# ScalarE makes the masked scores of the attention two groups ahead, half before the factors and half behind them

## The reference, cut to what matters

```python
xs = (x @ W_src).reshape(N, HEADS, HID)
xd = (x @ W_dst).reshape(N, HEADS, HID)
a_src = jnp.einsum('nhc,hc->nh', xs, att_src)
a_dst = jnp.einsum('nhc,hc->nh', xd, att_dst)
e = jax.nn.leaky_relu(a_src[src] + a_dst[dst], NEG_SLOPE)
m = jax.ops.segment_max(e, dst, num_segments=N)
ee = jnp.exp(e - m[dst])
denom = jax.ops.segment_sum(ee, dst, num_segments=N)
alpha = ee / (denom[dst] + 1e-16)
msg = xs[src] * alpha[:, :, None]
out = jax.ops.segment_sum(msg, dst, num_segments=N)
```

## Time and profile before

| | us |
|---|---|
| median of 3 runs | 8418.5 (8417.85 to 8419.08) |
| the profiled execution: its own time | 8423.03 |
| its span, first to last instruction | 8421.2 |
| the attention in it | 7169 to about 8340 |

### The profile page before, as it was taken

How to read it: one execution, slowest core, us unless ns; L and a number is a source line. 1 busy time by engine, 2 the same in 40 slices (tenths; PEclk the granted TensorE clock), 3 DMA queues, 4 the chain that set the end, 5 groups by cost and what they waited for, 6 DMA issues and landing times. The chain is left out here.

```text
span 8421.2 us, 105716 instructions
## 1 busy us (share of the span) xinstructions
PE 5596.3 (66%) x23206; PEld 3877.0 (46%) x23206; DVE 5678.2 (67%) x15211; ACT 3349.2 (40%) x10636; POOL 6042.4 (72%) x6427
## 2 busy tenths in 40 slices
PE   5777746666666666776667775666655555788885
PEld 3444423333444444444444443444444444667664
DVE  8959138888666666666666665555544444888887
ACT  2333347777455552333333332000001111666665
POOL 2777767777677777777777777777777776766664
PEclk6555558888788888999899998888765666777877
DMA  2111144444222224444444445444433322211111
GB/s 75 59 57 59 59 117 119 119 119 120 74 63 63 63 61 143 119 119 118 125 132 119 119 119 130 124 116 116 116 84 62 62 61 56 53 48 49 49 48 38
DMA packets 632208, 749.11 MB, mean 89 GB/s; under 512 B 257044, under 2 KB 490152, under 8 KB 631448
## 3 DMA queue, kind: packets, MB, share of 16 engines
q0 software_dynamic: 239808, 572.66, 23.8%
q1 hardware_dynamic: 391496, 169.55, 8.0%
q10 hardware_dynamic: 272, 0.14, 0.0%
HBM read 617.05 MB, written 124.77 MB: 88 GB/s over the span
## 5 line engine op out<-in xcount | busy, mean ns | idle before, releaser
L824 DVE TENSOR_TENSOR acc<-acc,ps 128x256 f32 (+3 forms) x4704 | 1761.3, 374 | 1550.9 <-PE ps L1862 1254.2
L1145 POOL DMA_INDIRECT rows<-table_gcn,index_dst x1984 | 1889.1, 952 | 671.7 <-issue 570.9
L1862 PE MATMUL ps<-rows,hot 128*128 128x256 f32 (+2 forms) x5536 | 1506.2, 408 | 1254.3 <-DMA rows<-table_gcn,index_dst 467.6
L1862 PEld LDWEIGHTS ps<-rows,hot 128*128 128x128 f32 x5536 | 1097.3, 244 | 1652.6 <-issue 719.7
L1756 ACT ACTIVATE ut<-u,fld 128x128 f16<-128x128 f16 x1568 | 541.9, 392 | 1532.9 <-DVE u L1804 1531.8
L1145 POOL DMA_INDIRECT rows<-table_gat,index_dst x832 | 784.9, 943 | 379.6 <-issue 239.3
L1145 POOL DMA_INDIRECT rows<-table_mean,index_src x784 | 741.3, 946 | 249.2 <-issue 234.4
L1145 POOL DMA_INDIRECT rows<-table_lin,index_dst x784 | 739.9, 944 | 247.5 <-issue 234.7
L1114 PE MATMUL ps<-prod,hot 128*128 128x257 f32 x1568 | 592.1, 494 | 365.6 <-DVE acc L824 197.2
L1847 PE MATMUL ps<-prod,ut 128*128 128x392 f16 x3136 | 741.2, 365 | 0.0
L1145 POOL DMA_INDIRECT hot_v<-table_gcn,index_dst x576 | 548.3, 952 | 175.5 <-issue 163.6
(11 more groups left out here) (428 smaller groups left out, 11017.7 us busy)
## 6 DMA issues: line engine op xcount, KB each, us to landing
fld<-dst_rows SPq DMA_DIRECT2D x98, 544.0 KB
rows<-table_gcn,index_dst POOLq DMA_INDIRECT x1984
table_gcn<-acc SPq DMA_DIRECT2D x147, 128.0 KB
fld<-left_rows SPq DMA_DIRECT2D x147, 128.0 KB
pay<-dst_rows SPq DMA_DIRECT2D x832, 1.0 KB
rows<-table_gat,index_dst POOLq DMA_INDIRECT x832
rows<-table_lin,index_dst POOLq DMA_INDIRECT x784
rows<-table_mean,index_src POOLq DMA_INDIRECT x784
```

Source lines behind the costliest of these rows:

```text
L824: c.nc.vector.tensor_tensor(to, to, product, ALU.add).then_inc(c.added.sem, 1)
L1145: pool.indirect_dma_start(to(q, j), None, table, bass.IndirectOffsetOnAxis(ap=c.idx[k][:, t:t + 1], axis=0)).then_inc(c.gathered[q % per]. ...
L1862: pe.matmul(c.ps[:, bank(q, j), 0:used], c.hot[:, r % 2, j, :], row_of(c, s, r, j, used), start=True, stop=True).then_inc(c.mm.sem, 1)
```

## The change

ACT's body begins with the two exponentials of group q. Then stand `turned` of q+1, `mask8` and quarters 0 and 1 of group q+2, the factor of q+1, and quarters 2 and 3 of group q+2. Before the loop it makes all four quarters of group 1. Since `mask8` can now be written sooner after its last reader, it waits for that reader (`scaled` of the group before). No instruction's shape or number changes, and the other engines keep their order.

```diff
@@ masked @@
                 if b == 0:
                     act.wait_ge(c.hot_ready.sem, q + (c.hot_ready.n + 1))
+                    if not first(q):
+                        act.wait_ge(m.scaled.sem, q * 4 + m.scaled.n)
                     nc.scalar.activation(s.mask8[:, :, :], hot_of(r), ACT.Copy, scale=-1.0,
@@ body of ScalarE @@
                 q = RING * i + r
-                if nxt(i, r):
-                    for b in range(3):
-                        masked(*nxt(i, r), b)
                 act.wait_ge(m.scored.sem, q + (m.scored.n + 1))
                 nc.scalar.activation(weight8, s.z[:, :, :], ACT.Exp).then_inc(m.powered.sem, 1)
                 nc.scalar.activation(heads(s.wt)[:, :, :, CH], s.z[:, :, :], ACT.Exp).then_inc(m.kept.sem, 1)
                 if nxt(i, r):
-                    masked(*nxt(i, r), 3)
-
                     turned(*nxt(i, r))
+                for b in range(2):
+                    if nxt(i, r, 2):
+                        masked(*nxt(i, r, 2), b)
+                if nxt(i, r):
                     factor(*nxt(i, r))
+                for b in range(2, 4):
+                    if nxt(i, r, 2):
+                        masked(*nxt(i, r, 2), b)
@@ before the loop @@
             turned(0, 0)
             factor(0, 0)
+            for b in range(4):
+                masked(0, 1, b)
             written_out(AG, body, RING)
```

## The result

| | before | after |
|---|---|---|
| median of 4 runs | 8418.17 us (8416.84 to 8419.08) | 8345.67 us (8341.48 to 8350.73) |
| ratio, 95% interval | | 0.9911 [0.9900, 0.9923] |
| the profiled execution: time, span | 8423.03, 8421.2 | 8345.77, 8344.0 |

The kernel is 72.5 us faster, or 0.9%. The forecast was 8379.6, with a range from 8350 to 8398. The direction was right and the size was not: the gain is nearly twice the 38.9 us of the sum, and the time lies 4 us beyond the range. A repeat of the changed kernel on another chip gave 8342.63, so this is no accident of one run.

What follows compares the result with a forecast made beforehand. The prediction took a ring through DVE and ACT, with twelve blocks before the exponential, to set the attention's pace. Terms -47.7 + 0.5 + 0.3 + 8 = -38.9 us gave 8384.1, or 8379.6 us as a median; range 8350 to 8398.

Steps and rivals of the forecast that it cites:

- the ring: Attention's pace: product on DVE, maxima, `drop`, factor, mask, twelve blocks, exponential, product; mean step 11.22 us.
- The wait for the exponentials, -47.7 us: DVE's product: its 47.9 us of waits for ACT's exponentials go, all but the last group's 0.2 us.
- PE comes next: Quarter 0 of PE's transposes: at low clock some 0.25 us late for DVE's maximum, in up to 65 groups; plus 8 us.
- The start, +0.3 us: Start of the attention: first exponentials stand behind four more ACT blocks, so the first product comes 0.3 us later.
- the fetches, +0.5: POOL's queue: rows are needed one group earlier; 0 to 3 us allowed in the first dozen groups, 0.5 taken.
- ACT free in time, by 1.2 us: ACT's queue: blocks done by T + 8.5, next scores ready at T + 9.7 (T: product's start), leaving 1.2 us.
- The loss as half of the throttled time: PE's clock: the skill's rule would give 234 us lost; the prediction read 34 us from DVE's waits instead.
- the clock stays up: Rival: PE's idle spells behind ACT's blocks go and its clock never falls; -81 us, 8337; chance 0.15.
- The rival of the slower look-up: PE's look-up at low clock takes 1.6 us more, DVE waits 1.5; up to 8468; chances 0.14 part, 0.04 slower.

Runs made afterwards that it cites:

- e3: Changed kernel with all four quarters of ACT's blocks put behind the factor, none in front: 8547.00 us.
- e11: The changed kernel run once more, on the same chip as e9: 8342.63 us.
- e10: e4 with DVE's maximum of quarter 1 moved in front of its product: 8385.85 us against e4's 8446.27.
- e4: Changed kernel in which DVE makes four eighths of each one-hot matrix twice, about 0.7 us more DVE work a group: 8446.27 us.
- e2: Changed kernel with all four quarters of ACT's blocks for the group after next in front of the factor: 8344.02 us.
- e5: Changed kernel with three unread transposes added on PE between quarters 2 and 3 in each group: 8343.50 us.
- e9: Changed kernel with DVE's maximum of quarter 1 moved in front of its product, behind that of quarter 0: 8325.18 us.
- e6: Kernel before with three unread transposes added on PE between quarters 2 and 3 in each group: 8418.52 us.
- e8: Changed kernel in which DVE makes one eighth of each one-hot matrix twice, about 0.3 us more a group: 8392.47 us.
- e7: e4 with three unread transposes added on PE between quarters 2 and 3 in each group: 8437.05 us.
- e1: Kernel before, still one group ahead, with two quarters of ACT's blocks before the exponentials and two behind, not three and one: 8408.67 us.

## Why the prediction was right or wrong

- **The bound and the ring: right.** e3 lengthened the ring and the step grew as worked out; the changed kernel's timeline has the new order of events at the times laid out.
- **The wait for the exponentials, -47.7 us: right in kind, too small.** It went completely, but a full-clock group lost 0.64 us (10.83 to 10.19) and its recorded wait was 0.53. The record of the maximum before the product runs 0.08 us past the point at which the next instruction can start. The sum counted idle time from the end of that record. About 100 times 0.08 us is 8 us, and DVE's busy time in the attention, in which overlapping records count once, fell by 1034.61 - 1025.45 = 9.2 us, of which the shorter product (1212 in place of 1223 ns, 104 times) is 1.1. The Trainium skill, "Perfetto Trace Analysis", section "Summary: the profiler window per engine type", says that a record of VectorE runs until the write is acknowledged; the trace agrees, in that the next instruction starts 0.08 us before the record's end.
- **"PE comes next", +8 us: wrong, and this is the step that failed.** It said that falls of the clock stay as frequent at the same place, and that some of their cost is newly paid at quarter 0. Measured instead: behind the first groups no maximum but the fourth waits at all, so nothing is paid at quarter 0; and the fourth waits in 22 groups in place of 65. The maxima's waits fell by 23.5 us (41.6 to 18.1), and the look-up's waits rose by 0.9 (5.5 to 6.4). The term should have been about -23. Together with the 8 us above it makes up the difference: -47.7 - 8 - 23.5 + 0.9 = -78.3, against the 78.0 measured between the first and the last product. (That the two agree to 0.3 us is partly luck: idle spells too short to be printed grew by about 3 us before the maxima, and smaller changes make up for it.) The price at quarter 0 was misread as well. The prediction lets its transposes begin where the look-up's record ends, at 7832.24; in the trace of before they begin at 7832.09:

```profile
7832.09 0.63 PE L2432 MATMUL ps<-ident,hot_v 128*128 128x128 f32 x4
```

With 1.08 us at low clock they end at 7833.17, 0.07 us behind the start of the maximum and not 0.25.
- **The start, +0.3 us, and the fetches, +0.5:** the start was right: from ACT's first block to the first product it is 15.33 us in place of 15.11, 0.2 more. The fetches cost nothing: ACT's blocks waited 1.4 us for one, as before, at the first group only. That the first product came 0.8 us later (7185.3 in place of 7184.5), as much as both terms together, is luck: the other 0.6 us is a later start of the whole attention, which moves by microseconds from one execution to the next (in e11, the same kernel, the first product comes at 7182.3).
- **ACT free in time, by 1.2 us:** it waits 1.25 us in the group shown. Right.
- **The loss as half of the throttled time:** this rule of the Trainium skill, from "TensorE: Matmul & The Clock Gate", section "HAM oscillation — how this bites in real kernels", stood in the prediction against 34 us of waits. In this kernel the low clock has a price only where PE is waited for: e10 at 0.84 pays nearly nothing at the maxima, and e4 at 0.79 pays 44 us. The measurement stands against the rule here too.
- **The rival "the clock stays up"** (chance 0.15, 8337) is nearest to what happened: a gain beyond 52 us, though the clock did not stay up. It gave the removed spells behind ACT as the cause. e4 rules that out: the spells stay away and the waits come back. What the waits follow is the length of a group. As DVE's work grows from 0 to 0.3 to 0.7 us more, the waits grow from 18 to 35 to 52 us. Over all kernels, the groups of 102 in which quarter 3 takes over 0.9 us number 16 to 23 at steps of 10.2 to 10.5 us (changed, e2, e5, e9, e11), 50 to 65 at 10.8 to 11.2 (before, e6, e8, e10), and 74 to 82 at 11.3 and more (e3, e4, e7). Only e1 stands out, with 89 at 11.08; its quarter 3 waits for ACT's blocks. More work on PE did not undo it (65 to 56 in e6, 74 to 82 in e7). A slow quarter 3 itself adds half a microsecond to a group, so part of this is the effect and not the cause. In the 10.25 us group shown above the clock is 1.00 until 2.5 us behind the product, where quarter 3 is just done, and then 0.50; seven groups in a row, from 7939.2 on, have a step of 10.24 or 10.25 us and a clock of 0.83, and no such wait. Why groups of this length let the clock fall behind quarter 3 and not in front of it isn't settled, and that the length is the cause is not shown beyond this: no kernel changed the length of a group and kept what PE does and waits for in it.
- **The rival of the slower look-up:** look-up waits grew by 0.9 us. It did not come about. (Its 1.6 us is right, but comes from the look-up's weight loads at full clock, 1.86 us; 3.49 less the 1.95 that it names would be 1.5.)

## What to carry to other kernels

When one engine does work ahead for another, look at what stands in its queue between the last thing that it waits for and the first thing that others wait for; that piece closes a ring, and moving work out of it pays even where the engine is busy for no more than 63% of the stage. In this kernel a low clock on PE is paid only where another engine waits for PE's result at once: find that place, and put work of the waiting engine beside it (e9), rather than fill PE to lift the mean clock (e5, e6). And a gap that the trace prints is a lower bound: here 0.08 us of waiting lay under the end of a record and as much again in spells too short to be printed. Over a hundred groups that was 8 us at the product and 15 at the fourth maximum, as much as many of the waits shown.

## What the hardware showed that I had not expected

The time depended on the length of a group by more than the work added, by way of PE's clock: 0.3 us more work a group, some 30 us, cost 47. The 128x1024 product on DVE takes 1212 ns behind another instruction and 1223 ns after a wait, by the medians of the changed kernel and of the earlier trace rows; e3 and e6, where it waits, have 1223 too, and the kernels where it doesn't wait 1211 to 1214. More work on PE raised its mean clock from 0.81 to 0.86 in the kernel before and bought no time: 8418.52 us against 8420.23 on the same chip.
